# The rough score products of an image/text attention: 64 rows of the array in place of 128

## What is computed

```python
NH = 16; HD = DIM // NH; IMG_LEN = 257
def attention(q, k, v):
    scale = 1.0 / jnp.sqrt(jnp.asarray(HD, q.dtype))
    scores = jnp.einsum('bqhd,bkhd->bhqk', q, k) * scale
    probs = jax.nn.softmax(scores, axis=-1)
    return jnp.einsum('bhqk,bkhd->bqhd', probs, v)
```

## Time and profile before

| | us |
|---|---|
| median of 3 runs | 3530.37 (3530.24 to 3533.05) |
| the profiled execution, its own time | 3520.77 |
| its span | 3519.0 |
| first and last R product issued | 1698.1 to 2217.5 |
| mean granted TensorE clock, share of full | 0.963 |

### The profile page before, as it was taken

The page is one execution under the profiler, slowest core; times in us unless marked ns, Lnnn a source line. Parts: engine busy times, 40 slices in busy tenths (PEclk is TensorE's granted clock), DMA queues, the critical chain, the costliest instruction groups (busy, mean ns, idle before and its releaser), DMA issues. The chain is left out here.

```text
span 3519.0 us, 63774 instructions
## 1 busy us (share of the span) xinstructions
PE 3264.8 (93%) x23076; PEld 2831.8 (80%) x23076; DVE 2333.8 (66%) x4613; ACT 2247.6 (64%) x5204; POOL 1561.2 (44%) x1568
## 2 busy tenths in 40 slices
PE   6758968999999999998899999897999999999989
PEld 5658957989989989997666665586999999999878
DVE  8976756776676676666777777435666655655554
ACT  3426746777777777775566676415777777777743
POOL 0003127777676667663121120103555555555534
PEclk8879979999999999998999999899999999999999
DMA  5206522211120120102101100213221121111011
GB/s 194 94 17 245 208 106 70 88 62 37 43 80 31 37 92 31 37 25 83 43 1 39 38 1 1 78 39 117 78 81 61 43 74 43 69 60 36 27 40 40
DMA packets 74456, 227.81 MB, mean 65 GB/s; under 512 B 7780, under 2 KB 29472, under 8 KB 69152
## 3 DMA queue, kind: packets, MB, share of 16 engines
q1 hardware_dynamic: 67538, 184.04, 14.7%
q0 software_dynamic: 3696, 37.68, 2.8%
q10 hardware_dynamic: 2910, 2.01, 0.2%
HBM read 178.60 MB, written 45.11 MB: 64 GB/s over the span
## 5 line engine op out<-in xcount | busy, mean ns | idle before, releaser
L1199 PE MATMUL ps<-a_v_rows,a_ring 128*128 128x129 f32 (+1 forms) x7168 | 933.3, 275 | 7.4 <-DVE a_o_rows L1592 6.4
L1564 DVE SCALAR_TENSOR_TENSOR a_peak<-ps,a_k_rstd,a_peak 128x512 f32<-128x512 f32 (+1 forms) x768 | 572.4, 745 | 505.5 <-ACT a_ring L1301 502.3
L1199 PEld LDWEIGHTS ps<-a_v_rows,a_ring 128*128 128x128 f32 (+1 forms) x7168 | 876.6, 191 | 26.3 <-ACT a_ring L1316 6.1
L1301 ACT ACTIVATE a_ring<-ps,a_k_rstd 128x512 f32<-128x512 f32 (+1 forms) x896 | 615.2, 687 | 429.6 <-PE ps L1189 386.1
L1424 POOL TENSOR_TENSOR a_ring<-a_ring,a_negb 128x512 f32<-128x512 f32 (+1 forms) x506 | 649.9, 1306 | 236.9 <-ACT a_negb L1310 229.0
L1316 ACT ACTIVATE a_ring<-a_ring 128x512 f32<-128x512 f32 (+1 forms) x896 | 562.8, 631 | 41.2 <-DVE a_ring L1581 27.7
L1187 PE MATMUL ps<-a_qt,a_kt 128*128 128x512 f32 (+1 forms) x896 | 425.2, 475 | 21.6 <-DVE a_peak L1564 17.4
L1092 PEld LDWEIGHTS ps<-a_wr,a_ct 128*128 128x128 f32 (+1 forms) x2496 | 352.7, 188 | 49.7 <-issue 14.0
L1092 PE MATMUL ps<-a_wr,a_ct 128*128 128x256 f32 (+1 forms) x2496 | 371.2, 286 | 13.9 <-DMA a_ct<-ctx_lo 13.7
L1189 PE MATMUL ps<-a_qt,a_kt 128*128 128x512 f32 (+1 forms) x896 | 355.5, 397 | 0.0
L1188 PE MATMUL ps<-a_qt,a_kt 128*128 128x512 f32 (+1 forms) x896 | 354.4, 396 | 0.0
(11 more groups left out here) (462 smaller groups left out, 6008.4 us busy)
## 6 DMA issues: line engine op xcount, KB each, us to landing
a_wr<-a_w SPq DMA_DIRECT2D x96, 512.0 KB, 4.4
a_w<-a_wr SPq DMA_DIRECT2D x32, 512.0 KB, 3.9
a_wr<-a_w SPq DMA_DIRECT2D x48, 256.0 KB, 3.3
a_ct<-ctx_hi SPq DMA_DIRECT2D x8, 1090.0 KB, 5.5
a_ct<-ctx_lo SPq DMA_DIRECT2D x8, 1090.0 KB, 8.7
f_we<-in_f_experts SPq DMA_DIRECT2D x8, 1088.0 KB, 8.4
ctx_hi<-a_ct SPq DMA_DIRECT2D x4, 1602.0 KB, 5.4
ctx_lo<-a_ct SPq DMA_DIRECT2D x4, 1602.0 KB, 9.3
```

The lines of the kernel that those rows point to most:

```text
L1199: ins = pe.matmul(m.ps[:, 6 + i // 2, (i % 2) * 256:(i % 2) * 256 + VW], slot(n)[0:r, i * P:(i + 1) * P], v_rows[u // NG % 2][0:r, t, :], ...
L1301: act.activation(slot(n)[0:r, :], m.ps[0:r, SCORE_BANKS[n % 2], :], ACT.Copy, scale=k_rstd[0:r, g % 2, t:t + 1]).then_inc(kept, 1)
L1564: dve.scalar_tensor_tensor(out=peak[0:r, :], in0=m.ps[0:r, SCORE_BANKS[n % 2], :], scalar=k_rstd[0:r, u // NG % 2, t:t + 1], in1=(slot(n - ...
```

## The change

R takes the rows of its head alone, from the queries and from the keys, in place of all 128. The columns, the order of the tasks, the waits, the banks and every other instruction stay as they are. The rows left out hold zeros in the queries, so the products are the same. An R with `i = 0` uses partitions 0 to 63 and one with `i = 1` partitions 64 to 127.

```diff
@@ -3239,8 +3239,9 @@
                         pe.wait_ge(kx_done, nth[("KX", h, keys_of(k) - 1)])
                     if j == 0:
                         pe.wait_ge(qx_done, 2 * nth[("QX", h, 0)])
-                    pe.matmul(out[:, 0:e - a], qt[h % 2][:, hp, i * S + q * P:i * S + (q + 1) * P],
-                              kt[h % 2][:, hp, a:e], start=True, stop=True).then_inc(r_ready, 1)
+                    rows = slice(STK * i, STK * (i + 1))
+                    pe.matmul(out[:, 0:e - a], qt[h % 2][rows, hp, i * S + q * P:i * S + (q + 1) * P],
+                              kt[h % 2][rows, hp, a:e], start=True, stop=True).then_inc(r_ready, 1)
```

## The result

The changed kernel takes 3617.5 us (median of 4 runs, 3610.8 to 3617.6) against 3531.1: a ratio of 1.024, 95% interval 1.0225 to 1.0255, 86 us slower. The prediction had the sign, but said 3581 and at most 3606.

A forecast was written before the change was run, and what follows sets the result against it. PE's issue sequence was taken to bound the turns. Switches 73.6, less 17.1 for overlap and 5 absorbed in idle time, gave +51.5, taken as +51: 3581 us from a median of 3530.4, range 3548 to 3606.

The forecast's parts named there:

- What bounds the kernel: In the turns, what PE issues sets the length; ACT and DVE wait for PE, PE for neither.
- A change of rows is a switch: Around R in the turns: 380 new switches, 0.20 us into R, 0.20 or 0.18 out, 73.6 us more.
- The sign named for it: From first score load to first R load in a turn: 0.52 us in place of 0.34.
- R KX R: Turn with R between other work: 0.20 us into each R, 0.18 out before KX; 0.4 to 0.8 longer.
- The 15-row transpose: Line 1068, another stage: its load's delay taken as evidence that rows alone cost a switch, 0.12 us each.
- The overlap: Neighbouring R in opposite halves within a run: partial overlap saves 17.1 us, bounds nothing and 29.7.
- a follower: An R directly behind another R in a run: 448 columns start after 0.107 in place of 0.205, saving 0.098 us.
- the 17.1: Overlap saving in us: 174 wide R that follow another R, 0.098 each.
- rival (4): Full overlap of neighbouring R: 73.6 - 29.7 - 5 = +39 us, 3569; chance 0.74 together with the forecast.
- the clock taken to stay at 1.00: In the turns, granted clock read as 1.00, the 2.4 GHz level; no term for losing it.
- Slots free in time: Ring of three slots for R: DVE needs 0.618 us for an R, 2.1 R a turn, so frees them in time.
- Ahead of the turns: The 32 R before the first turn, 8 runs: DVE the busier side, 0 booked, bounds 0 and 3 us.

The follow-up runs named there:

- e2: Kernel before, R at full height, with a short 64-row product ahead of R where it directly follows the scores (170 places): 3608.1 us, ratio 1.0212.
- e8: Changed kernel with 64 rows only in turns with one R or other PE work, and ahead of the first turn (330 R): 3600.3 us.
- e5: Kernel before, R at full height, with the products reordered head outermost as in e1: 3530.6 us, ratio 0.9993.
- e1: Changed kernel with the head index outermost, so 27 of 31 neighbours in a group lie in the same row half: 3645.5 us, ratio 1.0313.
- e3: Changed kernel, 64 rows, with each turn's R moved behind the turn's other work, only QB after them: 3628.6 us, ratio 1.0263.
- e4: Kernel before, R at full height, in the task order of e3: 3594.0 us, ratio 1.0164.
- e6: Kernel before, R at full height, with a 64-row product of 64 columns ahead of every run of R in the turns (261 places): 3641.8 us.
- e7: Kernel before with 64 rows only in the 73 turns whose PE work is two or three R and nothing else (182 R): 3535.1 us.
- e9: Changed kernel with a full-height copy of the first product ahead of each of the 261 runs of R in the turns: 3654.7 us.
- e10: As e6, but the added 64-row product has all the columns of its R (448 or 258) in place of 64: 3704.0 us, ratio 1.0506.

## Why the prediction was wrong

**What bounds the kernel: right.** PE's sequence sets the time; both readers only waited longer.

**A change of rows is a switch: right, and its price.** 0.20 us was taken; e2 shows 0.20. The sign named for it was wrong by its own parts: R's load 0.52 us behind the scores', where a load of 0.11, two products of 0.21 and a drain of 0.11 are 0.64; measured 0.66. In "R KX R" the three cost 0.49 where 0.58 was booked. The 15-row transpose was good evidence.

**The overlap: the mechanism right, the size wrong.** I took 0.098 for a follower, because loads of 128 columns were said never to start closer than 0.11 us. The earlier trace rows has four of KX in 0.40, the last 0.14, so 0.09 apart; that alone would have changed the 17.1 little. More: all loads in the rows were full height or alone. Loads of opposite halves start together, and a clean pair saves 0.19. That is rival (4): +39 forecast, 34 to 35 measured.
The Trainium skill ("TensorE: Matmul & The Clock Gate", Part 3) has packed tiles start about 4 ns apart. The two loads in 0.19 us agree, and the prediction should have weighed it higher.

**The step that failed: the clock taken to stay at 1.00, a term put at nothing.** I read it from the earlier trace rows and never priced its loss, though the change halves the rows of 512 products and puts idle time between them. The runs showed 126 us more at 1.2 GHz in its place: 52 of the 86 us by the medians, 41 of the 76 that the turns lost in the trace. Without it the change costs some 34 us, 3565, inside the range.

**Slots free in time: right for two and three R, wrong for four.** The one turn of four R at full clock costs 0.20 us more at half height (in e8 too), where two overlaps should have paid for more than its switch. Its fourth load waits for a bank, before and in the changed kernel:
```profile
2210.89 0.19 PEld L3242 LDWEIGHTS ps<-a_kt,a_qt 128*128 128x128 f32 x1 [0.69 <-DVE a_parts L3618]
```
```profile
2300.94 0.18 PEld L3243 LDWEIGHTS ps<-a_kt,a_qt 64*128 64x128 f32 x1 [0.89 <-DVE a_parts L3619]
```
It waits until DVE has reduced the first R, and the first comes some 0.2 us later than at full height, so the overlap gains nothing there.

**Ahead of the turns: right.** The turns begin at 1737 us in the changed kernel and at 1723 in the earlier trace rows, but in e5, at full height, they begin at 1737 as well. The other runs begin them between 1729 and 1739. So the early start seems to belong to that one execution of the kernel before, and with it the 9.6 us between it and the median.

**Still open.** Shown: the clock falls with R in halves, in three orders against the same order at full height (changed and before, e1 and e5, e3 and e4), with or without pairs (e1); much less with as many or more switches and R whole (e2, e6), and hardly where halves stand only in clean turns (e7). Not settled: what in the mixed turns it takes beside them; e7 also has fewer halves than e8 (182 against 330), so place and number are not told apart. And of the 86 us between the medians the traces place 76 in the turns; the other 10 are placed by none. Filling with full-height work hardly helped (e9), and whether the length of the half-height product matters e10 leaves open.

## What to carry to other kernels

A product that leaves the full array for part of its rows costs 0.20 us on entering and about as much on leaving, and two neighbours in opposite halves give 0.19 back: it needs runs of at least two, between work that changes shape anyway, to come out even. Count the runs in the issue order, not the products. And when a change halves the rows of products in a stretch that runs at 2.4 GHz and is bound by TensorE, put the loss of that clock among the rivals, and price it at 0.4 us for each us at half speed as here.

## What the runs showed of the hardware

- Weight loads of opposite row halves run at once (two in 0.19 us); of the same half 0.11 us apart (e1). Products on them run at once too, into different banks: a clean turn of two R is as long as at full height, and 0.19 us longer in e1.
- A switch of rows costs 0.20 us (e2), of which some 0.12 are drain; the drain seen before a switch of columns was 0.11 us.
- The time at 1.2 GHz differs between executions of one program: e1 448 or 569 us, e10 from 324 to 455, e8 from 352 to 684. With a kernel near such a fall, one profile can mislead by 50 us.
